# Attention values of two heads accumulated into one block of 32 rows, with zeros for the other head

## The reference

```python
qr, kr, vr = (to_regions(q), to_regions(k), to_regions(v))   # (B, 49, 64, C)
logits = jnp.einsum('brc,bsc->brs', qr.mean(2), kr.mean(2))
_, idx = jax.lax.top_k(logits, 4)
kg = take(kr, idx)                                           # (B, 49, 256, C)
vg = take(vr, idx)
...
scores = jnp.einsum('brqhd,brkhd->brhqk', qh, kh) * scale
attn = jax.nn.softmax(scores, axis=-1)
out = jnp.einsum('brhqk,brkhd->brqhd', attn, vh)
```

## Time and profile before

| | |
|---|---|
| median of 3 runs | 5610.56 us (5608.67 to 5612.54) |
| the profiled execution | 5625.85 us, of which span 5623.2 us |
| TensorE busy | 4720.9 us, 84% of the span |
| VectorE busy | 3648.9 us, 65% |
| ScalarE busy | 3287.3 us, 58% |
| GpSimd busy | 2777.4 us, 49% |
| mean granted TensorE clock | 0.898 of full speed |

### The profile page before, as it was taken

One profiled execution on the slowest core, in us unless ns is written; L12 is line 12 of the kernel. 1 busy time (PEld: TensorE's weight loads), 2 busy tenths in 40 slices (PEclk: granted clock), 3 DMA queues, 4 the chain that ended last, 5 costly groups with the idle time before them and its releaser, 6 DMA issues.

```text
span 5623.2 us, 182695 instructions
## 1 busy us (share of the span) xinstructions
PE 4720.9 (84%) x43666; PEld 3049.9 (54%) x43666; DVE 3648.9 (65%) x8855; ACT 3287.3 (58%) x6282; POOL 2777.4 (49%) x9656
## 2 busy tenths in 40 slices
PE   2388888888889898888888889888888888888888
PEld 1265555655556555555555556555565655556564
DVE  2266666766667666676766667666676766667676
ACT  1156556565665756556565665656556565665657
POOL 1245455454554645455454554545455464554553
PEclk9589899988889989898989999989899998999989
DMA  2333343333423334243333423334233333423311
GB/s 61 95 99 92 82 109 75 94 84 91 108 68 102 82 93 103 72 109 83 96 87 89 109 69 101 82 94 104 71 110 88 94 84 92 111 65 106 83 45 33
DMA packets 626961, 494.05 MB, mean 88 GB/s; under 512 B 483792, under 2 KB 613968, under 8 KB 615536
## 3 DMA queue, kind: packets, MB, share of 16 engines
q10 hardware_dynamic: 335360, 212.04, 16.6%
q1 hardware_dynamic: 290416, 268.94, 16.5%
HBM read 268.80 MB, written 211.94 MB: 85 GB/s over the span
## 4 chain that ended last, share of the span: by engine, by line
PE 52%; DMA 13%; issue 9%; ACT 7%; DVE 6%; DVEq 4%; SPq 4%; ACTq 3%; POOL 2%; POOLq 0%
PE ps L1003 11%; PE ps L1033 9%; PE ps L1017 8%; DMA max_d<-tr 6%; PE ps L896 5%; DMA qm<-qk_d 3%; DVEq L223 3%; PE ps L953 3%; ACTq L237 2%; PE ps L989 2%; PE ps L916 2%; PE ps L912 2%; DMA xin<-in_x 2%; ACT pt L847 2%; PE ps L974 2%
## 5 line engine op out<-in xcount | busy, mean ns | idle before, releaser
L736 DVE TENSOR_REDUCE mx<-ps 128x4 f32<-128x1024 f32 x1568 | 1921.6, 1225 | 1396.2 <-PE ps L1003 1128.7
L847 ACT ACTIVATE pt<-ps 128x512 f32<-128x512 f32 x3136 | 1694.2, 592 | 875.0 <-PE ps L1017 811.9
L505 POOL COPY vg<-vs 64x72 f32 x6272 | 1563.5, 249 | 781.6 <-POOL kg L490 576.7
L1003 PE MATMUL ps<-kg,qm 96*128 96x256 f32 x6272 | 1358.3, 342 | 364.4 <-DVE mx L736 112.2
L490 POOL CAST kg<-ks 96x128 fp32r x3136 | 845.2, 295 | 1550.5 <-PE ps L1017 1195.5
L1003 PEld LDWEIGHTS ps<-kg,qm 96*128 96x128 f32 x6272 | 963.3, 206 | 1087.2 <-issue 889.0
L1017 PE MATMUL ps<-qm,kg 97*128 97x256 f32 x6272 | 1126.5, 303 | 151.7 <-ACT pt L847 96.9
L1033 PE MATMUL ps<-pt,vg 128*32 128x128 f32 x25088 | 1092.0, 294 | 51.8 <-DVE um L726 39.1
L1017 PEld LDWEIGHTS ps<-qm,kg 97*128 97x128 f32 x6272 | 940.2, 206 | 214.6 <-ACT pt L847 154.7
L1033 PEld LDWEIGHTS ps<-pt,vg 128*32 128x32 f32 x25088 | 629.5, 114 | 296.5 <-issue 58.0
L645 DVE CAST kg<-ks 96x128 fp32r x3136 | 630.9, 244 | 137.9 <-issue 132.4
(11 more groups left out here) (113 smaller groups left out, 4036.1 us busy)
## 6 DMA issues: line engine op xcount, KB each, us to landing
qk_d<-stg SPq DMA_DIRECT2D x224, 448.0 KB, 3.6
qm<-qk_d ACTq DMA_DIRECT2D x1792, 42.0 KB
ks<-qk_d ACTq DMA_DIRECT2D x96, 784.0 KB, 6.3
vs<-v_d ACTq DMA_DIRECT2D x64, 882.0 KB, 7.1
xin<-in_x SPq DMA_DIRECT2D x119, 224.0 KB, 2.6
xi_d<-xi SPq DMA_DIRECT2D x112, 224.0 KB, 2.7
qk_d<-stg SPq DMA_DIRECT2D x112, 224.0 KB, 3.2
max_d<-tr SPq DMA_DIRECT2D x1568, 2.0 KB
```

Source lines behind the costliest of these rows:

```text
L505: j = pool.tensor_copy(vg[slot][rows, (k // 2) * VW:(k // 2 + 1) * VW], vs[place(m)[0]][rows, bass.ds(region, 1), :].rearrange("p o n -> p ...
L736: v.tensor_reduce(mx[h % 2][:].rearrange("p (g j e) -> p g j e", g=2, j=2)[:, :, :, 0], ps[:, 0:2, :].rearrange("p g (j k) -> p g j k", j= ...
L847: act.activation(pt[m % 2][:, c], ps[:, 2 + c, :], ACT.Exp, scale=float(HD) ** -0.5).then_inc(S["pt_ready"], 1)
L1003: i = pe.matmul(ps[:, g, 256 * j:256 * j + 256], qm[c % 2][0:NP3, t, g, 2 * j:2 * j + 2, :].rearrange("p h t -> p (h t)"), kg[slot][0:NP3, ...
```

## The change

The values lose the two columns of ones in DRAM and in `vs` (VW goes from 72 to 64). The ring tiles `vg` get a layout of 34 columns for each head pair (VC = 34): 8 values of the first head, 8 zeros, 8 values of the second head, a one, zeros, and a one in column 33. Zeros and ones are written once at the start; GpSimd's copies fill the two runs of 8. `attended` now makes one matmul for each head e: a window that begins at column 0 or 8, and only the 64 columns of `pt` of that head. Both heads add up into the same 64 columns of the same 32 rows: the first window has zeros in the rows of the second head's values, and the other way round. The sums come out in rows 24 and 25 of a block, where `pick` now looks for them; rows 16 to 23 and 26 to 31 hold numbers that nobody uses. ScalarE copies the finished block and signals `um_ready` itself; `second_heads`, the mask and the semaphore `u_ready` go.

```diff
-VC = 18
-VW = 4 * VC
+VW = C
+VC = 34
+VG = 4 * VC
...
-        vg = [sb(f"vg{i}", [128, 2 * VW + 16]) for i in range(RING)]
+        vg = [sb(f"vg{i}", [128, 2 * VG + 8]) for i in range(RING)]
...
-                    j = pool.tensor_copy(vg[slot][rows, (k // 2) * VW:(k // 2 + 1) * VW],
-                                         vs[place(m)[0]][rows, bass.ds(region, 1), :].rearrange("p o n -> p (o n)"))
+                    dst = vg[slot][rows, (k // 2) * VG:(k // 2 + 1) * VG].rearrange("p (j w) -> p j w", w=VC)[:, :, 0:32]
+                    j = pool.tensor_copy(dst.rearrange("p j (e x) -> p j e x", e=2)[:, :, :, 0:HD],
+                                         vs[place(m)[0]][rows, bass.ds(region, 1), :].rearrange("p o (j e d) -> p (o j) e d", j=4, e=2))
...
-            v.memset(vstg[:], 1.0)
...
-                v.memset(t[:], 1.0)
+                link(v.memset(t[:], 0.0))
+                for e in range(2):
+                    v.memset(t[:, 0:2 * VG].rearrange("p (a w) -> p a w", w=VC)[:, :, 24 + 9 * e], 1.0)
...
-                            j = v.tensor_copy(vstg[d, m0:m1].rearrange("p m i (j c) -> p (m i j) c", c=VC)[:, :, 0:16],
-                                              ps[d, 6, 128 * m0:128 * m1].rearrange("p (a c) -> p a c", c=16))
+                            j = v.tensor_copy(vstg[d, m0:m1].rearrange("p m i n -> p (m i n)"), ps[d, 6, 128 * m0:128 * m1])
...
-                m = h - PV_LAG
-                if live(m, kind) and group_end(m):
-                    second_heads(p, m)
...
-                    act.activation(merged(m, u), ps[:, 4, 0:128 * u].rearrange("p (u e t) -> p u e t", u=u, e=2)[:, :, 0], ACT.Copy).then_inc(S["u_ready"], 1)
+                    act.activation(merged(m, u), ps[:, 4, 0:RT * u], ACT.Copy).then_inc(S["um_ready"], 1)
...
-                for c in range(2):
+                for c, e in ((0, 0), (0, 1), (1, 0), (1, 1)):
                     for j in range(4):
-                        i = pe.matmul(ps[32 * j:32 * j + 32, 4, 128 * u:128 * u + 128],
-                                      vg[slot][:, c * VW + VC * j:c * VW + VC * j + 32],
-                                      pt[m % 2][:, c, 128 * j:128 * j + 128], start=c == 0, stop=c == 1)
+                        w, n = c * VG + VC * j + HD * e, 128 * j + RT * e
+                        i = pe.matmul(ps[32 * j:32 * j + 32, 4, RT * u:RT * u + RT], vg[slot][:, w:w + 32],
+                                      pt[m % 2][:, c, n:n + RT], start=c + e == 0, stop=c + e == 2)
```

More of the change, by code:

```diff
@@ L109, in build @@
         pick = sb("pick", [128, 128])
-        second = sb("second", [128, 1])
-        parts = sb("parts", [128, 8])
         mean_w = sb("mean_w", [128, 128])
@@ L170, in build @@
             reg_full reg_ready logit_full lg_ready top_ready topi_ready
-            kd_ready kp_ready vg_ready sm_full mx_ready tr_ready st_full pt_ready u_full u_ready um_ready
+            kd_ready kp_ready vg_ready sm_full mx_ready tr_ready st_full pt_ready u_full um_ready
             sum_full lns_ready rcs_ready un_ready y_full x2_ready xc2_full sq2_ready var2_full lnv2_ready rs2_ready
@@ L190, in merged @@
             strip = um0[:, r // NW] if i == 0 else um1[:, r // NW % 2]
-            return strip[:, t0:t0 + u * RT].rearrange("p (u t) -> p u t", u=u)
+            return strip[:, t0:t0 + u * RT]
         def settled(eng):
@@ L457, in _ @@
                 w = span.stop - span.start
-                pool.affine_select(out=v[:, :, span], in_=v[:, :, span], compare_op=ALU.not_equal, fill=1.0, base=-16 - e,
+                pool.affine_select(out=v[:, :, span], in_=v[:, :, span], compare_op=ALU.not_equal, fill=1.0, base=-24 - e,
                                    pattern=[[-32, 4], [0, w]], channel_multiplier=1).then_inc(Z, 1)
@@ L601, in _ @@
             v.tensor_copy(center_r[:], center_w[:])
[L602 to L605, removed]
             v.wait_ge(S["w_loaded"], 16 * WEIGHT_DMAS)
@@ L718, in finish @@
                         v.scalar_tensor_tensor(ot[:, b], ps[:, 5, 0:ST], blast, x2[:, b], ALU.add, ALU.add).then_inc(S["ot_ready"], 1)
[L720 to L727, removed]
             def step(p, h, kind):
```

## The result

| | before | changed |
|---|---|---|
| median | 5611.55 us (4 runs) | 5558.85 us (4 runs, 5544.52 to 5569.91) |
| ratio | 1 | 0.990 (95% interval 0.9866 to 0.9934) |
| the same in a later series, other chip | 5620.69 us (23 runs) | 5547.98 us (5 runs); 0.9875 (0.9846 to 0.9905) |

The change makes the kernel faster by 1.0%, 53 us; 5572 us (0.993) was forecast. The profiled execution of the changed kernel took 5569.85 us with a span of 5568.0, against 5625.85 and 5623.2.

A forecast was written before the change was run, and what follows sets the result against it. The prediction took TensorE, busy 84% of the span, as nearest to the bound. Its terms, -25 - 19 - 9 - 25 + 37 + 2 = -39 us, gave 0.993 or 5572 us on the median, with a range of 5490 to 5720.

The forecast's parts named there:

- the three terms of the chain through VectorE: TensorE's waits for merged rows, the maximum and the MLP's copies, shortened by removing VectorE's copy: -25, -19 and -9 us.
- the value loads: Value loads shrink from 882 to 784 KB and land 0.8 us earlier, so maxima queue less: -25 us, bounds 0 to 51.
- the passes: In `attended` on TensorE, 32 passes of 64 columns replace 16 of 128: +37 us, bounds 5 to 216.
- the start: Changed fills before the first loads of weights can start: about +2 us.
- TensorE's waits merely change their names: Sign of being wrong: TensorE's waits would only move elsewhere; no size given.
- The wait for the merged rows: TensorE's 54 waits before `attended`, 39.1 us, nearly all end but partly return at what is next: -25 us.
- VectorE's time: VectorE freed of 896 copies, shortening TensorE's waits for the maximum by 19 us and for the MLP's copies by 9.
- Small edits: ScalarE's copy and VectorE's copy of projected values cost nothing more; fills at the start cost about +2 us.
- A pace of one pass in 27 ns: Rival: pass rate, not columns, limits `attended`: +564 us, some 6090; chance 0.19, shared with sets above 0.062 us.
- The dearer copies: Rival: GpSimd's value copies cost up to 440 ns, short steps wait for keys: +260 us, about 5830; chance 0.05.
- The larger gains: Rival: TensorE's waits for VectorE go with little paid again, passes cost 20: -125 us, about 5485; chance 0.18.
- the four terms: Merged rows 39, maximum 37, MLP's copies 18 and value loads 51 us at full size, 145 us together.

The follow-up runs named there:

- the runs with the chain in place: Kernel before with narrow values and 64-column passes, predicated copy kept: 0.9951; changed kernel with the predicated copy put back and waited for: 0.999.
- the kernel before with another start: Kernel before with 14 small fills and seven waits more at VectorE's start, nothing else: 5625.34 us, 1.0011.
- the runs with and without somebody who waits: Predicated copy on VectorE: waited for, 0.999 (changed kernel) or 0.9951 (kernel before, narrow values, short passes); on constants in the changed kernel, nobody waiting, 0.9923.
- its time put back: Changed kernel with a predicated copy of the old size back on VectorE, on constants into a spare tile, nobody waiting: 5580.42 us, 0.9923.
- with the chain back: Changed kernel with the predicated copy back between ScalarE's copy and the merged-rows signal, narrow values and 64-column passes kept: 5619.7 us, 0.999.

## Why the prediction was right, and where it was not

The forecast was 5572 us with a range of 5490 to 5720; measured 5558.85. The sum was -39 us against -53 (-70 in the later series, against whose changed kernel the parts are measured). In its two halves it came out so: the three terms of the chain through VectorE, -53 together, measure -43 to -65 by the runs with the chain in place; the value loads, the passes and the start, +14 together, measure about -5 to -28. So the main term had the right size, and the rest the wrong sign by an amount small enough to leave the total right. That part is luck, and so in part is the size of the main term, because it was summed from waits that the traces do not show to have gone.

**The premise.** "What the removed copy can give back must lie in these three" waits, the prediction says. The three (for the merged rows, for the maximum, for the MLP's copies) were 277.3 us before and are 251.2 after, a fall of 26 where 53 were taken; in the kernel before with another start they are 266.7. And TensorE's whole idle time fell by 11 us in one profile of the changed kernel and by nothing in the other, while its busy time fell by 44 and 49. The prediction had no term for the clock, and it is there that the gain shows. "TensorE's waits merely change their names" was its own sign of being wrong: of the waits that is close to what happened, and yet the kernel is faster. How the shorter chain leads to a higher clock, no run isolates.

The terms one by one:

**The wait for the merged rows.** It should end at nearly every one of 54 places; it ended at all of them (39.1 us to 0.0). 25 us were taken; the runs with and without somebody who waits give 16 or 38, by the kernel they are held against. That the wait would end was right. That TensorE pays for it at the next waits was right too, and not careful enough: idle time of 51.8 us went at this place and 49.3 us came at the scores and the turned scores. So the time that the runs show was not gained as idle time of TensorE, and the 25 us as the prediction derives them are not confirmed.

**VectorE's time.** 19 + 9 = 28 us were taken, and its time put back costs some 27. The size is right, the reason given for it is not shown: the waits in which it should appear, TensorE's for the maximum and for the MLP's copies, did not fall (127.3 and 123.9 us against 112.2 and 126.0). With the work put back they are 141.7 and 133.6, 20 to 24 us above the changed kernel's two profiles, which is in keeping with the reason; but the first of them alone differs by 17 us between the kernel before and the same with another start. The runs say that freeing VectorE helps; where on TensorE's path it does so stays open.

**The value loads.** 25 us were taken from a landing 0.8 us earlier. It lands 0.4 us earlier (6.7 against 7.1), and the waits for the maxima rose in the changed kernel. Alone the part measured -21 us, with short passes nothing. A gain within the bounds (0 to 51) at best, and not shown to come the way that was told.

**The passes.** The term of the sum that failed: +37 us, in truth nothing or below. The set of four passes was taken at 0.057 us and is 0.055, and the shorter end of the last pass, which I left out of the sum as no gain, gives 0.054 us a step. So `attended` is 0.01 us longer, not 0.028, and that over 1568 steps and 0.84 would be 13 us. The run with nothing but short passes was 35 us faster. "A gain is left out, because the columns are the same in number" is the sentence that failed: the clock is not the same. It was 0.906 with 32 passes and 0.900 with 16, and by the 28 us for 0.01, which is a correlation, that goes with some 18 of the 35 us; the rest is not accounted for.

**Small edits.** The fills put the first wait for weights at 18.56 us; in the trace before it is 17.25. That is 1.3 us against the 2 that were taken. The lines are the last fill of VectorE, before and then after:

```profile
17.25 0.11 DVE L597 MEMSET mean_w<- 64x64 f32 x1
```

```profile
18.56 0.11 DVE L599 MEMSET mean_w<- 64x64 f32 x1
```

GpSimd's copies took 243 ns against 242 forecast. No run copies 64 columns in one run of columns, so that the breaks cost nothing rests on the forecast's slope and on the 242 ns of four runs of 16.

**The rivals.** A pace of one pass in 27 ns is refuted, by 14 ns here and 9 ns with 32 columns. The dearer copies did not come. The larger gains came in part: the sum of the four terms at their full size was 145 us, and 53 to 70 were measured. Three signs that the prediction named as proof failed though the time was right: the wait for the maximum did not fall below 112.2 us, that for the maxima in DRAM rose to 347 rather than fall to 230, and the value load lands after 6.7 us, not 6.3. Three came: `attended`'s matmuls without a longer busy time, the wait for the merged rows under 15 us, GpSimd's copies at 243 ns.

## What to carry to other kernels

A predicated copy that only picks between two results of the same matmul can be saved by zeros in the stationary operand; with four column blocks side by side, twice as many passes of 64 fp32 columns cost the matrix engine 0.01 us a step, while passes of 32 do cost. That a wait has gone from its line says nothing of what is gained: add up the engine's busy and idle time over the whole span, before and after, and look whether the idle time has moved to another line (here 51.8 us went and 49.3 came). Measure the parts by putting back the work without the wait, and the wait with it, and hold the result against more than one form of the kernel: one neighbour gave 38 us here and the other 16. And before trimming 8 of 72 columns off a transfer, ask what queues behind it: splitting the transfer in two was worth more than all of the change.

## What the runs showed of the hardware

**The granted clock rose with the number of short passes.** With the same columns: 0.898 to 0.902 in the kernels with 16 passes a step, 0.903 to 0.913 with 32, 0.927 with 64 (all without halved loads). In the last the kernel had 172 us more of pace on TensorE and was 60 to 70 us slower than with 32. That short passes keep the clock up is in keeping with all of these runs. They don't isolate it: in the 32-pass kernels the clock also rises as waits go (0.903 with the chain back, 0.913 without), so waits seem to act too, and the shares are not known. It rises with halved loads as well, to 0.919 with 16 passes and to 0.920 and 0.928 with 32.

**Halving the loads of keys and values and spreading them** took about 2% off either kernel, by far the largest effect seen. The small ones here are the maxima of 2 KB, 1568 times there and back.
